# Second cross attention of a Perceiver block on one NeuronCore: values and probabilities in a high and a low part, weighed in one-pass products for two pairs of heads at a time, and exponentials in two tiles in place of four

## The reference, cut to what matters

```python
xn = _layernorm(x, ln1_w, ln1_b)              # context: 16 x 1601 x 128
latn = _layernorm(latents, ln2_w, ln2_b)      # 16 x 64 x 128
q = latn @ Wq
kv_input = jnp.concatenate([xn, latn], axis=1)
k, v = jnp.split(kv_input @ Wkv, 2, axis=-1)
weight = jnp.einsum('bhld,bhnd->bhln', q * scale, k * scale)   # 16 heads
weight = jax.nn.softmax(weight, axis=-1)
out = jnp.einsum('bhln,bhnd->bhld', weight, v)
return out.transpose(0, 2, 1, 3).reshape(b, l, INNER) @ Wo
```

## Time and profile before

| | us |
|---|---|
| runs | 2008.15 median of 3 (1999.8 to 2008.78) |
| profiled execution, its own time | 2003.31 |
| its span, from first to last instruction | 2001.5 |
| PE busy | 1738.1 (87% of the span) |
| DVE busy | 1240.1 (62%) |
| ACT busy | 854.5 (43%) |
| POOL busy | 521.2 (26%) |

### The profile page before, as it was taken

The page is one execution under the profiler, slowest core; times in us unless marked ns, Lnnn a source line. Parts: engine busy times, 40 slices in busy tenths (PEclk is TensorE's granted clock), DMA queues, the critical chain, the costliest instruction groups (busy, mean ns, idle before and its releaser), DMA issues. The chain is left out here.

```text
span 2001.5 us, 33395 instructions
## 1 busy us (share of the span) xinstructions
PE 1738.1 (87%) x11692; PEld 1227.9 (61%) x11692; DVE 1240.1 (62%) x3068; ACT 854.5 (43%) x1931; POOL 521.2 (26%) x707
## 2 busy tenths in 40 slices
PE   5799999999977898279999999999999999999423
PEld 2466666666655787256676766667666676675322
DVE  5466666666643665466666666666666666654477
ACT  2255565655541333144444444444444444443222
POOL 1001000000001221234334543245433354310123
PEclk9699999999997898689999999999999999999665
DMA  4335344444410011210000000000000000000000
GB/s 108 95 86 114 95 106 102 112 100 101 92 51 0 22 62 45 92 52 11 28 18 28 27 16 22 17 27 27 27 11 17 27 27 27 1 1 1 0 5 5
DMA packets 32659, 90.35 MB, mean 45 GB/s; under 512 B 8552, under 2 KB 17424, under 8 KB 32528
## 3 DMA queue, kind: packets, MB, share of 16 engines
q1 hardware_dynamic: 32528, 88.71, 16.5%
HBM read 40.43 MB, written 8.91 MB: 25 GB/s over the span
## 5 line engine op out<-in xcount | busy, mean ns | idle before, releaser
L2016 PE MATMUL c_pv_ps<-c_prob_t,c_xn 128*128 128x512 f32 (+2 forms) x896 | 411.7, 596 | 0.0
L340 ACT ACTIVATE c_prob<-c_score_ps,c_neg_max 128x512 f32<-128x512 f32 (+1 forms) x512 | 304.3, 607 | 64.6 <-PE c_scratch L2002 35.0
L871 DVE TENSOR_REDUCE a_chunk_max<-a_side_ps 128x1 f32<-128x512 f32 (+1 forms) x416 | 260.8, 665 | 109.3 <-PE a_side_ps L692 109.1
L359 DVE TENSOR_REDUCE c_chunk_max<-c_score_ps 128x1 f32<-128x512 f32 (+1 forms) x512 | 291.0, 581 | 47.2 <-PE c_score_ps L266 45.6
L237 PE MATMUL c_turn_ps<-consts,c_prob 128*128 128x128 f32 (+2 forms) x1792 | 286.2, 277 | 12.1 <-DVE c_prob_t L369 11.3
L237 PEld LDWEIGHTS c_turn_ps<-consts,c_prob 128*128 128x128 f32 (+2 forms) x1792 | 212.3, 139 | 98.1 <-issue 32.4
L2016 PEld LDWEIGHTS c_pv_ps<-c_prob_t,c_xn 128*128 128x128 f32 (+2 forms) x896 | 157.8, 190 | 163.5 <-issue 163.4
L373 DVE COPY c_prob_t<-c_turn_ps 65x128 f32<-65x128 f32 (+1 forms) x256 | 61.5, 280 | 298.0 <-PE c_turn_ps L237 298.0
L804 ACT ACTIVATE a_prob<-a_st_ps 128x1024 f32<-128x1024 f32 (+1 forms) x224 | 214.4, 958 | 66.8 <-PE a_st_ps L676 66.8
L266 PE MATMUL c_score_ps<-c_x_hi,c_q_hi 128*128 128x512 f32 (+1 forms) x512 | 218.5, 427 | 2.4 <-ACT c_prob L340 1.6
L324 ACT ACTIVATE c_prob_t<-c_turn_ps 128x512 f32<-128x512 f32 x128 | 76.4, 597 | 277.5 <-PE c_turn_ps L237 276.1
(11 more groups left out here) (288 smaller groups left out, 2640.9 us busy)
## 6 DMA issues: line engine op xcount, KB each, us to landing
a_stack<-a_k_hi SPq DMA_DIRECT2D x128, 200.1 KB, 4.1
a_stack<-a_k_lo SPq DMA_DIRECT2D x64, 200.1 KB, 4.2
a_ctx<-in_ctx_dram SPq DMA_DIRECT2D x16, 768.0 KB
c_ctx<-in_ctx_dram SPq DMA_DIRECT2D x16, 768.0 KB
absorbed_queries<-b_q_out SPq DMA_DIRECT2D x16, 512.0 KB, 3.6
c_q_raw<-absorbed_queries SPq DMA_DIRECT2D x16, 512.0 KB, 3.3
w<-in_L_ffn_w_dram SPq DMA_DIRECT2D x2, 512.0 KB
f_raw<-in_L_xattn_Wkv_dram SPq DMA_DIRECT2D x2, 512.0 KB, 5.1
```

Source lines behind the costliest of these rows:

```text
L340: nc.scalar.activation(prob[s % 2][:, cols], score_ps[:, cols], ACT.Exp, bias=neg_max[:, s % 2:s % 2 + 1], accum_out=sums[:, (s // QUAD) % ...
L359: nc.vector.reduce_max(chunk_max[:, s % 2, c:c + 1], score_ps[:, quad_chunk(c, keys)], AX_X).then_inc(chunk_max_done, 1)
L871: nc.vector.reduce_max(out, rows, AX_X).then_inc(side_taken, 1)
L2016: last = nc.tensor.matmul(lay.own.pv_ps[:], t.xn[m][0:rows, i, :], lay.own.prob_t[u][0:rows, i, :], start=(i == 0), stop=(i == LAT))
```

## The change

Values and probabilities are each kept as a rounded part and a rest, both in the type of one-pass products: `v_hi`, `v_lo` (new, made by POOL in `split_rows` at the end of `pool_prepare`) and `p_hi`, `p_lo` (in place of `prob_t`; ACT writes every `p_hi` from PSUM, DVE subtracts it from the same PSUM bank to give `p_lo`). The weighing goes by a **duo** of two pairs: 14 tiles times three products of 256 columns, seven tiles in each of two slots, so 21 products in every slot. `xn` has one buffer in place of two. The exponentials of a pair are two tiles (1,024 and 641 columns), its maxima three (1,024, 512 and 129), and the two short transposes are copied as one piece of 65 rows. The jobs move: `norm` to slots 1 and 5, `out` to slot 3, and the reciprocal sums and the scaling of a quad (`finish_quad`) to other slots accordingly.

```diff
-    half = [None] * 7 + [("norm",), None, xt[0], xt[1], None, xt[2], None, xt[3], ("norm",)]
-    lay.jobs = [half[:11] + [("out",)] + half[12:], half]
+    half = [None] * 3 + [("norm",)] + [None] * 5 + [xt[0], xt[1], ("norm",), xt[2], None, xt[3], None]
+    lay.jobs = [half[:7] + [("out",)] + half[8:], half]
...
+        def split_rows(eng, ops, b, m, first, waits):
+
+            if not first:
+                wait_apart(eng, lay.own.pv_done, CHUNKS * QUADS * (b - 1), waits)
+            wait_apart(eng, t.xn_done, CHUNKS * (b + 1), waits)
+            for c in range(CHUNKS):
+                for rows, tiles in (((P, slice(4 * c, 4 * c + 4)),) if c < 3 else ((TAIL, slice(FULL, FULL + 1)), (SEQ, slice(LAT, LAT + 1)))):
+                    last = ops.tensor_copy(t.v_hi[m][0:rows, tiles, :], t.xn[0:rows, tiles, :])
+                last.then_inc(t.v_high, 1)
+            for c in range(CHUNKS):
+                eng.wait_ge(t.v_high, CHUNKS * b + c + 1)
+                for rows, tiles in (((P, slice(4 * c, 4 * c + 4)),) if c < 3 else ((TAIL, slice(FULL, FULL + 1)), (SEQ, slice(LAT, LAT + 1)))):
+                    last = ops.tensor_tensor(t.v_lo[m][0:rows, tiles, :], t.xn[0:rows, tiles, :], t.v_hi[m][0:rows, tiles, :].bitcast(F32), ALU.subtract)
+                last.then_inc(t.v_split, 1)
...
             normed_rows(pool, nc.gpsimd, b, (m + 1) % 2, first, t.pool_waits)
+            split_rows(pool, nc.gpsimd, b, (m + 1) % 2, first, t.pool_waits)
...
             for i in tiles:
-                if i < len(lay.tiles):
-                    rows = lay.tiles[i][0]
-                    last = nc.tensor.matmul(lay.own.pv_ps[:], t.xn[m][0:rows, i, :], lay.own.prob_t[u][0:rows, i, :],
-                                            start=(i == 0), stop=(i == LAT))
+                rows = lay.tiles[i][0]
+                out, v_hi, v_lo = lay.own.pv_ps[:, DUO * P * u:DUO * P * u + DUO * P], t.v_hi[m][0:rows, i, :], t.v_lo[m][0:rows, i, :]
+                nc.tensor.matmul(out, v_lo, lay.own.p_hi[u][0:rows, i, :], start=(i == 0), stop=False)
+                nc.tensor.matmul(out, v_hi, lay.own.p_hi[u][0:rows, i, :], start=False, stop=False)
+                last = nc.tensor.matmul(out, v_hi, lay.own.p_lo[u][0:rows, i, :], start=False, stop=(i == LAT))
...
             if what[0] == "norm":
 
-                pe.wait_ge(diag_done, 4 * k + (s - 7) // QUAD + 1)
+                pe.wait_ge(diag_done, 4 * k + (s - 5) // QUAD + 1)
...
             if part == 0:
-                pe.wait_ge(copied_dve, (q + 1) * QUAD * 3)
-                pe.wait_ge(copied_act, (q + 1) * QUAD)
-                if not (isinstance(q, int) and q == 0):
+                pe.wait_ge(low_done, (e + 1) * DUO * CHUNKS)
+                if i % 2 == 0 and not (isinstance(q, int) and q == 0):
                     pe.wait_ge(pv_taken, q)
...
-                i, part = (s // QUAD - 1, s % QUAD - 1) if s % QUAD else (s // QUAD - 2, CHUNKS - 1)
+                i, part = ((s - 3) // 2, 0) if s % 2 else ((s - 4) // 2, 1)
...
-                maximum(k, s, 0)
-                lay.dve_between(dve, k, kind, s, 0)
                 if s and (s - 1, "a") in table[kind]:
                     lay.dve_take(dve, table[kind][s - 1, "a"], base(kind, k), k, kind, s - 1)
+                if s >= 2 or kind != "first":
+                    low_halves(k, s - 1, 3)
+                lay.dve_between(dve, k, kind, s, 0)
                 if before:
-                    copy_turned(k, kind, s, 0)
-                for c in range(1, CHUNKS):
-                    maximum(k, s, c)
-                    if c < CHUNKS - 1:
-                        lay.dve_between(dve, k, kind, s, c)
+                    low_halves(k, s, 0)
+                maximum(k, s, 0)
+                lay.dve_between(dve, k, kind, s, 1)
+                if before:
+                    low_halves(k, s, 1)
+                maximum(k, s, 1)
+                lay.dve_between(dve, k, kind, s, 2)
+                maximum(k, s, 2)
...
-                if s % QUAD == 1 and not (kind == "first" and s < QUAD):
+                if s % QUAD == 0 and not (kind == "first" and s < QUAD):
                     denominators(4 * k + s // QUAD - 1, (s // QUAD - 1) % 2)
-                if s % QUAD == 0 and not (kind == "first" and s < 2 * QUAD):
-                    finish_quad(k, s // QUAD - 2, own.number_after(k, kind, s - 1, "a"))
+                if s % QUAD == 2 and not (kind == "first" and s < QUAD + 2):
+                    finish_quad(k, s // QUAD - 1, own.number_after(k, kind, s - 1, "a"))
                 lay.dve_extra(dve, k, kind, s)
```

More of the change, by code:

```diff
@@ L39 @@
 SLOTS = 2 * PAIRS
+DUO = 2
+DUOS = SLOTS // DUO
 LN_EPS = 1e-5
@@ L92, in number_jobs @@
                 finishes = job is not None and job[0] in ("norm", "out")
-                if job is None or (kind == "first" and finishes and s < 7) or (kind == "last" and m == 1 and not finishes):
+                if job is None or (kind == "first" and finishes and s < 5) or (kind == "last" and m == 1 and not finishes):
                     continue
@@ L210, in _ @@
         body(BODIES - 1, "last")
-        make_diag(2 * BATCH - 1, own.number_after(BODIES - 1, "last", 15, "a"))
+        make_diag(2 * BATCH - 1, own.number_after(BODIES - 1, "last", 13, "a"))
     @block.tensor
@@ L229, in turn @@
             first = kind == "first" and s == 1
[L230 to L235, removed]
+            if c >= 2 or not first:
+                pe.wait_ge(low_done, CHUNKS * pair + c - 1)
             for i, (rows, col) in enumerate(groups[c]):
+                rows = rows if c < 3 else TAIL
                 last = nc.tensor.transpose(turn_ps[c % 2][0:rows, P * i:P * i + P], prob[(s - 1) % 2][:, col:col + rows], ident)
@@ L288, in _ @@
         body(BODIES - 1, "last")
+        pe.wait_ge(exp_done, BATCH * PAIRS * 2)
         for c in range(CHUNKS):
-            pe.wait_ge(exp_done, (BATCH * PAIRS - 1) * CHUNKS + c + 1)
             turn(BODIES, "mid", 0, c)
[L293 to L296, removed]
+        weigh_values(BODIES, -2, 1)
+        weigh_values(BODIES, -1, 0)
+        job(("norm",), base("last", BODIES - 1) + len(table["last"]), 0, "mid", BODIES, 1)
+        weigh_values(BODIES, -1, 1)
         if lay.last_output:
-            job(("out",), base("last", BODIES - 1) + len(table["last"]) + 1, 0, "mid", BODIES, 5)
+            job(("out",), base("last", BODIES - 1) + len(table["last"]) + 1, 0, "mid", BODIES, 3)
     @block.scalar
@@ L426, in _ @@
         body(BODIES - 1, "last")
-        for c in (0, 1, 3):
-            copy_turned(BODIES, "mid", 0, c)
+        low_halves(BODIES, -1, 3)
+        for c in range(CHUNKS):
+            low_halves(BODIES, 0, c)
         denominators(2 * BATCH - 1, 1)
-        finish_quad(BODIES, -2, own.number_after(BODIES - 1, "last", 15, "a"))
         finish_quad(BODIES, -1, base("last", BODIES - 1) + len(table["last"]) + 1)
@@ L1991, in pe_job @@
                 b = 0 if kind == "start" else 2 * k + m + 1
-                par = 0 if kind == "start" else (m + 1) % 2
                 pe.wait_ge(t.xn_done, CHUNKS * b + c + 1)
@@ L1995, in pe_job @@
                     c0 = col - BANK * c
-                    last = nc.tensor.transpose(own.scratch[:, c0:c0 + rows], t.xn[par][0:rows, 4 * c + i, :],
+                    last = nc.tensor.transpose(own.scratch[:, c0:c0 + rows], t.xn[0:rows, 4 * c + i, :],
                                                g.consts[0:rows, C_IDENT:C_IDENT + rows])
```

121 lines of the change are left out of this document (72 added, 49 removed).

## The result

The changed kernel took **2098.35 us** (median of 4 runs, 2088.82 to 2100.96), the kernel before 2004.88 beside it (4 runs). The ratio is 1.0457, with a 95% interval of 1.0418 to 1.0496: slower by 4.6%. The forecast was 2093, its range 2037 to 2140.

The account below looks back on a forecast made before the run. PE bounds the second cross attention at 61.1 us a batch; POOL's late diagonals make it 68.0. That gives +95 us between first and last `neg_max`, then -6 and +1: +90 on 2003.3, 2093 us, range 2037 to 2140.

Parts of the forecast that it names:

- The chain and the wait: POOL's power starts at 23.6 us, diagonals end at 51.1; PE, there at 42.6 or 46, waits 8.5 or 5, 15 times.
- The split: POOL's `split_rows`, ahead of the first quad's diagonals, costs 7.1 us a batch, between 6.4 and 7.8.
- PE's own work: One-pass products at 0.12 us each replace the records of values: 1.9 us less a quad, 62 us in 32 quads.
- The rival in which weight loads bind: PE's new products take 0.19 us each, a batch 72.7: +165 us, 2165; chance 0.04.
- The ring: From one slot's scores through maxima and exponentials to the next scores: 6.8 us instead of 5.6, 7.1 with DVE's statistics.
- slot 2: ACT's copy of `norm` delays the second exponential and short `p_hi`: some 0.55 us more, 7.7 for the slot.
- The clock: PE's clock halves for 3.4 to 5.9 us behind each wait, losing 2.2 us a batch, bounds 0 and 4.
- Sum: First to last `neg_max`: a first batch, 14 of 68.0 us and seven slots, 1065 against 970.3, so +95; +90 overall.
- The first batch and the last slots: First batch 66 us; seven last slots of 6.8 us without preparation, 47.6.
- the tail: Behind the last slot PE's value work falls from 13.8 to 7.6 us, -6, with +1 for transposes.
- Had the diagonals been in time: Rival: no wait at `norm`, a batch is its slots' sum, 56.8 us or 58.5 with `out`; 1956 us, chance 0.08.
- third rival: Weight loads bind PE's new products at 0.19 us each; a batch takes 72.7, +165 us, 2165; chance 0.04.

Follow-up runs that it names:

- e1: The changed kernel with POOL making the diagonals of a batch's first quad ahead of `split_rows`; 1985.15 us, 0.9911 of the kernel before.
- e2: The changed kernel with three more POOL subtractions per batch in the split, into a spare tile nobody reads; 2157.01 us.
- e4: The changed kernel with DVE's statistics that POOL waits for placed ahead of the scaling of the quad; 2076.71 us.
- e6: The changed kernel with the edits of e1 and e4 together; 1971.94 us, 0.9852 of the kernel before.
- e9: e6 with PE's six loop turns written out as straight code, so PE has no jump back; 1962.53 us.
- e7: e1 with the third product of each tile (high values by low probabilities) left out; 1943.28 us.

## Why the prediction was right

**The chain and the wait, the part that decides.** From the first scores of slot 0 (1338.13) in the batch shown, POOL's power starts at +23.4 (forecast 23.6) and the diagonals end at +50.5 (51.1). PE is there at +43.0 (42.6). It waits 7.5 and 4.4 us where 8.5 and 5 were forecast, 15 times; 89.9 us in all where about 100 were forecast. e1 shows the cause by taking away the place alone, e2 by making the chain longer, e4 by starting it earlier.

**The split.** Forecast 7.1, measured 6.6: a cast of 512 columns takes 0.56 from one to the next, a subtraction 1.22. The Trainium skill ("GPSIMD Engine Reference", section 3.1) would give some 1.12 for it by division, an estimate from that page; the measured pace lies between it and the 1.28 of the forecast, and nothing hung on the difference.

**PE's own work.** 0.12 a product was forecast; in the changed kernel they start 0.11 to 0.12 apart:

```profile
1378.57 0.28 PE L2057 MATMUL c_pv_ps<-c_p_hi,c_v_hi 128*128 128x256 f32 x1
1378.69 0.28 PE L2058 MATMUL c_pv_ps<-c_p_lo,c_v_hi 128*128 128x256 f32 x1
1378.81 0.28 PE L2056 MATMUL c_pv_ps<-c_p_hi,c_v_lo 128*128 128x256 f32 x1
1378.92 0.28 PE L2057 MATMUL c_pv_ps<-c_p_hi,c_v_hi 128*128 128x256 f32 x1
```

The rival in which weight loads bind (0.19) falls with it.

**The ring.** Forecast: `neg_max` at +5.3, next scores at +6.8; measured +5.4 and +6.86. With statistics 7.1 was forecast and 7.25 measured. The one step that was wrong in kind is slot 2, which ACT's copy of `norm` was to hold up to 7.7: it is 7.24 long (1352.62 to 1359.86). The two slots before it were 0.3 us longer than forecast together and slots 3 to 5 up to the wait 0.5, so that PE's arrival comes out near the forecast by cancelling.

**The clock.** 2.2 us a batch were taken. Two batches without a jump between them take 136.4 us in the changed kernel and 120.2 in e1; less the difference of the waits (11.9 against some 0.7) this leaves 5.0, so 2.5 a batch. From the first `neg_max` to the last the two differ by 113.2 us, 84.6 of it waits, which leaves 1.9 for each of 15. Half of the 4.8 us at half clock lies between.

**Sum.** Between the first and the last `neg_max` +95 was forecast, and it was +104.5. The 14 batches took 68.5 on average and not 68.0 (+7). Batches with `m` = 1 took 67.4 to 68.1; of those with `m` = 0, the one with no jump ahead of it 68.5, the five behind a jump 69.2 to 71.8. The pauses at the jumps, 6 us in all beyond the 68.5, are what the forecast did not have; more than half of it is the one batch of 71.8, behind the only pause of this kernel that half clock follows. The first batch and the last slots gave +2. The first `neg_max` came 2.2 later. In the other direction the tail behind the last one became 9.2 us shorter (forecast 5). Neither was looked into. The spans differ by 97.5 us and the medians by 93.5, where +90 was forecast, so 2093 is nearer to 2098 than the single terms are: the tail's surplus offsets a part of what the batches had too little.

**The rivals.** Had the diagonals been in time, the forecast gave 1956. e1 took 1985 and e6 1972: the side of that case was right and the gain too large. A part of e1's gain is the tail: of the 19 us between the spans, 9 lie behind the last `neg_max` and 9 between the first and the last. The forecast left out the pauses (9 us by e9) and had 58.5 for the mean batch, where e6 has 59.4 without a jump (57.9 and 60.9), mostly in the last three distances of a batch, 22.4 together where 21.2 was put. In the third rival 2003.3 and 165 make 2168 and not 2165, which changes nothing else.

## What to carry to other kernels

Work that is small against an engine's idle time (here 6.6 us in 68, on an engine that is busy for 45% of the stage) can cost more than its length if it stands in that engine's queue ahead of something short that the bounding engine waits for; follow the chain from what starts it to what consumes it, and put the short thing first. A change that gives PE less work can still lose by the waits, and here each wait of 4.4 us or more also cost half of the next 3 to 6. Where a loop's instructions grow by a third, as PE's records here, look at the queue that brings them and at the first instruction behind the jump back.

## What was not expected of the hardware

A PE loop turn of 16 slots with some 37 records of products a slot, or 43 (e7), shows no pause ahead of the turn's first scores and at most one packet of q8 in 600 us; one with 50 a slot shows 1.7 to 2.3 us of standstill at each of five jumps, at 36 to 43 packets. Half clock follows some of these pauses and not others: one of five in the changed kernel, two in e1, three in e6, none in e2. In e1 it does not follow the pause of 2.25 us that ends at 1094.37, and it follows the one of 1.82 that ends at 1339.03:

```profile
1095.00:1097.00 2.00, 2.00 (x15) 1.68 (x14) 0.57 (x1) 0.67 (x2) 0.00 (x0) 1.00 0.00 0
...
1340.00:1342.00 2.00, 2.00 (x8) 1.72 (x7) 0.19 (x1) 0.60 (x1) 0.00 (x0) 0.50 0.00 0
```

Straight code of the same length (e9) has neither: the clock is 1.00 where e6 has its pauses. The Trainium skill, "Runtime: NRT & Kernel Launch", section "Instruction fetch mechanics", says that a taken branch to code outside of what the engine holds makes it fetch that code before it can go on. The runs agree, with some 2 us for it. The page also says that "there's no instruction cache that benefits from spatial locality". The runs differ where that is read as a loop being fetched anew each turn: the loops of 37 and 43 records a slot went round with at most one packet of q8 in 600 us.
